# Identity products on TensorE ahead of each z and each batch's sums in the first edge pass of a graph network

## What is computed

```
x = concatenate([node_feats[src], node_feats[dst], edge_feats], axis=1)
m = maximum(x @ W1 + b1, 0.0) @ W2 + b2
return segment_sum(m, dst, num_segments=N_NODES)
...
x = _layernorm(x + _L0_gnn_ref(x, edge_attr_32, src, dst, L0_gnn_W1, ...))
x = _layernorm(x + _L1_gnn_ref(x, edge_index, edge_attr_16, ...))
x = _layernorm(x + _L2_gnn_ref(x, edge_index, L2_gnn_W, L2_gnn_a))
x = _layernorm(x + _L3_gnn_ref(x, src, dst))
```

## Time and profile before

| | |
|---|---|
| time of three runs | 5761.96, 5762.61, 5765.02 us |
| median | 5762.61 us |
| span of the profiled execution | 6618.7 us |
| first edge pass, POOL's gathers | from 94 to 2605 us of the span |
| second edge pass, POOL's gathers | from 2797 to 5193 us |
| TensorE busy over the span | 4926.0 us, 74% |
| POOL busy over the span | 4014.0 us, 61% |

### The profile page before, as it was taken

How to read it: one execution, slowest core, us unless ns; L and a number is a source line. 1 busy time by engine, 2 the same in 40 slices (tenths; PEclk the granted TensorE clock), 3 DMA queues, 4 the chain that set the end, 5 groups by cost and what they waited for, 6 DMA issues and landing times. The chain is left out here.

```text
span 6618.7 us, 104783 instructions
## 1 busy us (share of the span) xinstructions
PE 4926.0 (74%) x33518; PEld 3702.2 (56%) x33518; DVE 3854.6 (58%) x7688; ACT 1920.7 (29%) x4445; POOL 4014.0 (61%) x4125
## 2 busy tenths in 40 slices
PE   5566777777777776467777777777776469999689
PEld 4455666766667765356666566666655332222289
DVE  3122355555555542356666666666665469999855
ACT  1111222222222211112222222222211149999811
POOL 4555566666666665366666666666666627787634
PEclk6555566565565555555555555555555579999899
DMA  6644355555555544244444444444444334343298
GB/s 164 113 111 132 103 150 150 148 144 146 145 149 149 148 136 116 65 118 130 132 132 131 131 127 130 132 131 131 131 131 115 72 101 129 124 129 124 69 336 301
DMA packets 897045, 902.75 MB, mean 136 GB/s; under 512 B 635824, under 2 KB 779480, under 8 KB 880373
## 3 DMA queue, kind: packets, MB, share of 16 engines
q1 hardware_dynamic: 568404, 708.29, 33.9%
q0 software_dynamic: 115488, 115.45, 9.0%
q10 hardware_dynamic: 212608, 72.31, 4.8%
HBM read 656.88 MB, written 239.54 MB: 135 GB/s over the span
## 5 line engine op out<-in xcount | busy, mean ns | idle before, releaser
L507 POOL DMA_INDIRECT mlp_G<-mlp_src,src_cols x1612 | 1531.3, 950 | 1027.5 <-PE mlp_z L873 480.7
L507 POOL DMA_INDIRECT gatv_G<-gatv_src,src_cols x1612 | 1529.2, 949 | 940.1 <-DMA X<-in_x 435.7
L691 DVE TENSOR_TENSOR mlp_hots<-mlp_in_psum,src_lo 128x1024 bf16<-128x1024 bf16 x608 | 416.6, 685 | 734.3 <-remote 573.7
L909 PE MATMUL gatv_sums<-gatv_msg,gatv_same 128*128 128x68 f32 x3234 | 712.0, 390 | 151.7 <-issue 149.8
L909 PEld LDWEIGHTS gatv_sums<-gatv_msg,gatv_same 128*128 128x128 f32 x3234 | 688.2, 310 | 171.2 <-issue 169.1
L909 PE MATMUL mlp_sums<-mlp_zs,mlp_same 128*128 128x64 f32 x3234 | 676.5, 389 | 64.8 <-issue 64.6
L909 PEld LDWEIGHTS mlp_sums<-mlp_zs,mlp_same 128*128 128x128 f32 x3234 | 648.4, 301 | 66.0 <-issue 65.9
L2201 POOL TENSOR_TENSOR keys<-src_lo,gsoft_ring 128x512 f32<-128x512 f32 (+1 forms) x448 | 505.1, 1133 | 182.5 <-ACT src_lo L2344 172.7
L2266 PE MATMUL gsoft_acc<-keys,masks 128*64 128x512 f32 (+1 forms) x1568 | 558.2, 621 | 77.0 <-DVE keys L2440 42.1
L869 PE MATMUL gatv_z<-attr_w,gatv_attrT 112*128 112x448 f32 x462 | 422.3, 1017 | 206.3 <-DVE gatv_msg L597 107.9
L873 PE MATMUL mlp_z<-mlp_win,mlp_hot 128*128 128x64 bf16 x4851 | 384.6, 232 | 240.2 <-issue 236.2
(11 more groups left out here) (481 smaller groups left out, 8498.5 us busy)
## 6 DMA issues: line engine op xcount, KB each, us to landing
mean_block<-blocks SPq DMA_DIRECT2D x62, 1568.0 KB
gsoft_ring<-blocks SPq DMA_DIRECT2D x105, 896.0 KB
sums_gatv<-gatv_out_rows SPq DMA_DIRECT2D x231, 252.0 KB
mlp_rel<-rel_rows SPq DMA_DIRECT2D x116, 448.0 KB
gatv_rel<-rel_rows SPq DMA_DIRECT2D x116, 448.0 KB
sums_mlp<-mlp_out_rows SPq DMA_DIRECT2D x231, 224.0 KB
blocks<-masks SPq DMA_DIRECT2D x31, 1568.0 KB
blocks<-work SPq DMA_DIRECT2D x31, 1568.0 KB
```

The lines of the kernel that those rows point to most:

```text
L507: pool.indirect_dma_start(out=G[:, b.gq, j * L.gathered:(j + 1) * L.gathered], out_offset=None, in_=L.gather_table, in_offset=bass.Indirec ...
L691: last = nc.vector.tensor_tensor(hot_of[:, slot(b, k), :, :, :], bc(steps2_of[:, 0:w, :], 1, [P, OCTET // K2, w, K2]), bc(of_step[:, cols] ...
L909: last = pe.matmul(sums[b.q % 2][:, j * L.msg:(j + 1) * L.msg], same[:, b.q, j, :], rhs, start=True, stop=True)
```

## The change

In the first pass alone (`if not soft`) a helper `keep_busy(to, n)` multiplies the identity by an identity that is repeated four times, 512 bf16 columns wide, into the whole bank `to`, n times over. Each of them begins its bank anew, as does what follows, so nothing of them is left in the result. The helper is called at two places of a batch:

- in `make_z`, into the z bank that is written next: 6 times for a building batch, 8 for another;
- in `make_sums`, into the sums bank: 6 times for a building batch, 12 for another.

The wait that makes the bank free (`z_added` or `sums_copied` of batch b-2) is moved ahead of the identity products; the other waits stand behind them.

```
+            def keep_busy(to, n):
+                w = to.shape[1]
+                for _ in range(n):
+                    pe.matmul(to.rearrange("p (g e) -> p g e", e=P), S["ident_bf"][:, 0:to.shape[0]],
+                              bc(S["ident_bf"][:, :], 1, [P, w // P, P]), start=True, stop=True)
+
             def make_z(b):
+                wait(pe, act_done if soft else z_added, b.used(2))
+                if not soft:
+                    keep_busy(z[b.q % 2][:, :], 6 if builds(b) else 8)
                 wait(pe, hot_made, b.used())
                 wait(pe, win_in[b.q], b.landed(B))
-                wait(pe, act_done if soft else z_added, b.used(2))
...
             def make_sums(b):
+                wait(pe, sums_copied, b.used(2))
+                if not soft:
+                    keep_busy(sums[b.q % 2][:, :], 6 if builds(b) else 12)
                 wait(pe, masks_made, b.used())
...
-                wait(pe, sums_copied, b.used(2))
```

## The result

| | median us | runs |
|---|---|---|
| before | 5763.82 | 5761.96 to 5771.25, 4 runs |
| after | 5807.47 | 5804.89 to 5810.22, 4 runs |

The ratio is 1.007, with a 95% interval of 1.0056 to 1.0084: the change costs 44 us. The forecast was +59.

What follows compares the result with a forecast made beforehand. POOL's gathers, 8.75 us a batch, were taken to bound both edge passes. To the median 5762.6 us came +69 in the first 48 batches and -10 in building batches: 5821.6, forecast as 5820 us; 8-in-10 range 5695 to 5930.

Steps and rivals of the forecast that it cites:

- The long waits are mostly the profiler's: Both edge passes: 865 us of POOL's long waits match 856 us missing; without the profiler both run near 8.75 us a batch.
- Terms 1 and 2: Building batches 7.1 us instead of 8.6, 10 us gained in all; last 31 batches 7.6 instead of 6.0, nothing: POOL's 8.75 covers.
- Term 3: Batches 0 to 47 without groups (31): the products cost TensorE 1.6 us each, 50 us.
- Term 4: Batches 0 to 47 with groups (17): +3.3 us each, 56 us, of which perhaps 10 us come back.
- Term 5: Up to batch 48: 96 us more make TensorE's 445 us 541; POOL wants z at 472, so stands 69 us more.
- One sign: First 48 batches, changed kernel's profile: POOL's waits for z should be longer than the 137.9 us there were.
- Faster: Rival: TensorE bounds the building batches, say 9.4 us, and the change brings them to 8.75; 5694 us, chance 0.20.
- No change: Rival: waits for SP's rows and DVE in the first 48 batches hide the extra products; 5763 us, chance 0.20.
- Much slower: Rival: the clock stays low around the extra products; the first 48 batches alone give 6158 us; chance 0.08.

Runs made afterwards that it cites:

- fill_stalls: Kernel before plus three identity products of 384 columns ahead of each of 46 groups of turn_steps that wait for ACT's copies: 6617.74 us, ratio 1.001.

## Why the prediction was nearly right

The time (5807 us against 5820) and the sign were right, the place of the loss too. By its steps:

**"The long waits are mostly the profiler's".** Wrong in the cause, right in what follows. POOL's waits of 2.28 and 1.95 us are not there in a profile of 5777.5 us, and its pass is POOL's 8.75 us a batch. But the 6618.7 us are hardly the profiler's doing: on one chip the kernel takes 6609.91 us in 17 runs, and profiles of other kernels there, which add nothing to their times, have the same long waits. On which chip the first profile was taken is not known, so this is argued from the likeness. To count 865 us of waits against 856 us of missing time was sound; to say whose they were was not.

**Terms 1 and 2, building batches and the last 31: -10 us and 0.** Measured: products from batch 48 on change nothing (0.9998), so the cover was right. Under it, the 8.6 us that the products were to shorten was wrong. From batch 48 on TensorE is behind and catches up with POOL, and its own pace shows: the copies of batches 48 to 59 and the stretch in the columns of the earlier trace rows, before and then after:

```profile
L756 ACT ACTIVATE mlp_out_rows<-mlp_sums x12: 545/547/547, 616.2 to 688.9; 128x448 f32<-128x448 f32 x12
616.00:689.00 73.00, 60.70 (x799) 55.49 (x795) 63.52 (x125) 29.88 (x68) 55.11 (x59) 0.88 0.73 205
```

```profile
L756 ACT ACTIVATE mlp_out_rows<-mlp_sums x12: 545/547/547, 664.8 to 748.7; 128x448 f32<-128x448 f32 x12
664.00:749.00 85.00, 79.11 (x926) 61.54 (x924) 63.70 (x124) 31.18 (x70) 64.27 (x69) 1.00 0.65 180
```

A batch takes 72.7 / 11 = 6.6 us before and 83.9 / 11 = 7.6 us with the products (of which 0.5 are small waits, so the 7.1 us of the sum is right). Where TensorE sets the pace, its own work has the clock at 0.88 already; it is only later, where it stands for POOL, that the mean is 0.70. So the products cost TensorE 1.0 us a batch more than the clock returned, even here, where it rose to full.

**Term 3, batches without groups: 31 x 1.6 = 50 us.** This failed, in the price and in the path. The products there cost no time that shows (1.0002). Of batches 8 to 47 the 23 without groups take 19 us longer, 0.8 us each and not 1.6, and the 17 with groups 11 us less, as their first groups find the higher clock. What is left goes into time in which TensorE stood for windows before the next burst (6.37 and 3.29 us, in the rows above). In the sum I charged each batch its own price; only batches behind which TensorE does not stand until POOL asks should have been charged.

**Term 4, batches with groups: 56 - 10 = 46 us.** Right in the main: 39.5 us, with the products behind groups alone. The rows of after bear out its price, eight products at the low clock and twelve at the high one:

```profile
413.79 3.59 PE L860 MATMUL mlp_z<-ident_bf 128*128 128x512 bf16 x8
417.18 0.85 PE L877 MATMUL mlp_z<-attr_w,mlp_attrT 128*128 128x256 f32 x2
...
418.89 2.75 PE L860 MATMUL mlp_sums<-ident_bf 128*128 128x512 bf16 x12
421.49 1.67 PE L919 MATMUL mlp_sums<-mlp_zs,mlp_same 128*128 128x64 f32 x14
```

3.39 / 8 = 0.424 us and 2.60 / 12 = 0.217 us, against 0.44 and 0.22. The Trainium skill ("TensorE: Matmul & The Clock Gate", Part 1) gives 426.7 ns for 512 columns at the low clock, and the trace now agrees, with 0.424 us.

**Term 5, POOL's lead of 27 us (472 against 445).** This failed too, the other way. POOL stands 35.7 us for z in the first 48 batches of before already, so there was no lead to use up: 445 us was TensorE's work without its waits for windows and for DVE, 39.4 and 37.1 us from 91 to 680 us. What comes on top there counts, wherever TensorE does not stand afterwards.

So 59 - 50 + 27 - 6.5 + 10 = 39.5 (the last 10 are the gain of term 1, which did not come; the other 4 of the 44 us are within what the runs can tell): two wrong terms of opposite sign, 50 and 27 us, made up for each other in part. That the forecast is this near is in part luck; it is better than its reasons. One sign failed too: POOL's waits for z in the first 48 batches were to exceed 137.9 us and are 83.5, since the 137.9 belong to the execution of 6618.7 us. (Its first gather starts at 82 us, not at 94.)

**The rivals.** "Faster" needed building batches of over 9.2 us; they take 8.73. On the chip of 6609.91 us they take 10.69; the change was not run there, but with five gathers a batch its products cost 410 us. The rule that this rival leaned on, in the Trainium skill, "TensorE: Matmul & The Clock Gate" (the table "Why this matters for your kernels"), says to keep TensorE busy: the clock rose as it says, from 0.70 to 0.96, and no time came of it, since POOL's gathers set the pace. "No change" is what the 31 batches without groups did, in part for the reason given there (waits that the products fill). "Much slower" is excluded by the clock.

## What to carry to other kernels

A warm clock is worth what the engine that sets the pace gets of it, and products that only warm it have to be paid where TensorE is that engine: price them (0.22 us for 512 columns at the high clock) against half of the low-clock work that follows. And read the clock where that engine is really behind: here it was 0.88 there without any help, and 0.70 only in the mean. Look first for where the engine stands in the middle of its order; a second bank took 35 us off where all clock work took 7 at best. And before a sum is made against a profile whose span is far from the median, take another one: the difference may be the chip's.

## What the runs showed of the hardware

**Chips differ by 15%.** The same kernel takes 5764 to 5777 us on some and 6609.91 us on another. The stages after the second pass are as long on both (from its last gather to the end 1,427 us in the profile of 6618.7 us, 1,424 in that of 5777.5), and so are single operations; the two edge passes are longer. In the longer profiles several engines stand at once in the middle of a batch, TensorE even between products that wait for nothing. The second pass in the first profile of before, then the same place in the one of 5777.5 us:

```profile
3501.87 0.22 PE L909 MATMUL gatv_sums<-gatv_msg,gatv_same 128*128 128x68 f32 x1 [0.26 <-issue]
3503.28 0.89 PE L909 MATMUL gatv_sums<-gatv_msg,gatv_same 128*128 128x68 f32 x7 [1.19 <-issue]
3503.55 0.18 DVE L590 TENSOR_TENSOR gatv_diff<-gatv_logits,gatv_z 128x28 f32<-128x28 f32 x1 [0.74 <-remote]
3503.74 0.94 POOL L507 DMA_INDIRECT gatv_G<-gatv_src,src_cols  x1 [1.98 <-DMA X<-in_x]
```

```profile
3000.09 3.10 PE L909 MATMUL gatv_sums<-gatv_msg,gatv_same 128*128 128x68 f32 x14
3002.98 0.86 PE L946 MATMUL gatv_build_ps<-gatv_hots 128*128 128x49 bf16 x8
```

What stops them is not settled by any run here. Nor was the changed kernel itself run on such a chip.

**Few columns can raise the clock.** With twenty products of 64 columns in each of the first 48 batches the mean clock from 91 to 660 us was 0.69 instead of 0.59, and 0.83 with twenty of 512 columns. On the chip of 6609.91 us, in the kernels with five gathers, rows of 64 columns did little (0.74 instead of 0.71 from 760 to 2300 us).

**A busy TensorE can stay at the low clock.** The kernel with two banks, on a chip of the faster kind, with z and sums of two batches and four groups between them:

```profile
389.00:408.00 19.00, 19.00 (x112) 16.02 (x112) 4.69 (x7) 5.52 (x20) 14.43 (x16) 0.50 0.49 133
```

It stands nowhere in these 19 us, and the granted clock is 0.50 throughout; in fill_stalls it is the same over 26.5 us. So what raised the clock in the kernels with identity products is not just that the gaps were closed. What in them did, no run here separates.
